# First four adjacency blocks built and widened right behind layer zero, and normalised rows and roundings moved in the adjacency loop

## What is computed

```python
x = _layernorm(x + _L0_gnn_ref(x, src, dst, W_w, W_b, a_w, a_b), axis=-1)    # attention over edges
x = _layernorm(x + _L1_gnn_ref(x, edge_index, W), axis=-1)
x = _layernorm(x + _L2_gnn_ref(x, edge_index, edge_attr_4, ...), axis=-1)    # gated messages
x = _layernorm(x + _L3_gnn_ref(x, edge_index, edge_type_64, ...), axis=-1)   # typed messages

def _L1_gnn_ref(H, edge_index, W):
    new_H = segment_sum(H[src], dst, num_segments=H.shape[0])
    return relu((H + new_H) @ W)
```

## Time and profile before

| | us |
|---|---|
| median of 3 runs | 1089.4 |
| lowest, highest | 1089.07, 1090.24 |
| the profiled execution | 1089.84 |
| its span | 1088.0 |
| PE busy | 1002.6 (92%) |
| DVE busy | 861.1 (79%) |
| ACT busy | 691.3 (64%) |
| POOL busy | 218.2 (20%) |

### The profile page before, as it was taken

One profiled execution on the slowest core, in us unless ns is written; L12 is line 12 of the kernel. 1 busy time (PEld: TensorE's weight loads), 2 busy tenths in 40 slices (PEclk: granted clock), 3 DMA queues, 4 the chain that ended last, 5 costly groups with the idle time before them and its releaser, 6 DMA issues.

```text
span 1088.0 us, 27899 instructions
## 1 busy us (share of the span) xinstructions
PE 1002.6 (92%) x10463; PEld 874.7 (80%) x10463; DVE 861.1 (79%) x1934; ACT 691.3 (64%) x1489; POOL 218.2 (20%) x260
## 2 busy tenths in 40 slices
PE   3798979699999999995999999779999999989997
PEld 3343557599999999995788889669999999976775
DVE  6875999988998989987766677788787888766754
ACT  3467765454555555456888888577677776776554
POOL 4501340000000000000000000126666666610000
PEclk9899999899999999997999999889999999999998
DMA  6000020366767677752866564235444445334232
GB/s 159 1 2 1 4 68 3 121 207 225 238 215 225 222 238 227 204 175 72 292 195 193 172 201 141 82 104 140 138 136 129 131 131 139 109 112 124 69 99 82
DMA packets 86925, 150.38 MB, mean 138 GB/s; under 512 B 14524, under 2 KB 58375, under 8 KB 86557
## 3 DMA queue, kind: packets, MB, share of 16 engines
q1 hardware_dynamic: 65609, 116.01, 35.9%
q10 hardware_dynamic: 16122, 22.16, 5.7%
q0 software_dynamic: 5056, 10.36, 3.9%
HBM read 112.56 MB, written 35.94 MB: 136 GB/s over the span
## 4 chain that ended last, share of the span: by engine, by line
PE 81%; DVE 10%; ACT 4%; issue 3%; DMA 2%; POOL 0%; POOLq 0%; DVEq 0%; SPq 0%; ACTq 0%
PE PS L2500 14%; PE PS L2705 14%; PE PS L2488 11%; PE PS L2688 8%; PE PS L2611 7%; PE PS L2791 6%; PE PS L2581 3%; PE PS L2588 3%; PE PS L2326 2%; PE PS L2339 2%; DVE ring L1659 2%; DVE vo L1663 2%; PE PS L2403 2%; ACT X L1227 1%; PE PS L2357 1%
## 5 line engine op out<-in xcount | busy, mean ns | idle before, releaser
L1151 ACT CAST vo<-XT 128x768 f32<-128x768 bf16 (+1 forms) x218 | 180.3, 827 | 163.7 <-PE PS L2705 64.2
L984 POOL DMA_INDIRECT XT<-tab,ring x158 | 159.9, 1012 | 113.5 <-PE PS L2705 60.2
L2500 PE MATMUL PS<-vo 128*128 128x133 f32 x1300 | 175.9, 284 | 1.2 <-ACT vo L1151 1.2
L2500 PEld LDWEIGHTS PS<-vo 128*128 128x128 f32 x1300 | 157.2, 191 | 1.4 <-issue 1.4
L2488 PE MATMUL PS<-kp,ring 128*128 128x132 bf16 x1950 | 146.7, 221 | 3.2 <-DVE ring L1631 1.7
L2705 PE MATMUL PS<-vo 128*128 128x128 f32 x984 | 132.8, 279 | 0.0
L2488 PEld LDWEIGHTS PS<-kp,ring 128*128 128x128 bf16 x1950 | 125.6, 97 | 5.4 <-DVE ring L1631 1.8
L1641 DVE TENSOR_TENSOR XT<-iotab,XT 128x768 bf16<-128x768 bf16 (+1 forms) x218 | 120.0, 551 | 3.2 <-DMA hots_d<-XT 1.5
L2705 PEld LDWEIGHTS PS<-vo 128*128 128x128 f32 x984 | 118.9, 191 | 3.0 <-issue 2.4
L2490 PE MATMUL PS<-SDP,ring 128*128 128x12 bf16 x650 | 110.2, 170 | 0.0
L1286 ACT CAST adjf_r<-PS 128x512 fp32r<-128x512 f32 (+1 forms) x175 | 92.4, 550 | 25.4 <-PE PS L2581 23.6
(11 more groups left out here) (350 smaller groups left out, 2008.6 us busy)
## 6 DMA issues: line engine op xcount, KB each, us to landing
ring<-rows_d SPq DMA_DIRECT2D x146, 416.0 KB, 5.8
hots_d<-XT ACTq DMA_DIRECT2D x108, 192.0 KB, 4.7
big<-hots_d SPq DMA_DIRECT2D x10, 640.0 KB, 5.3
XT<-hots_d SPq DMA_DIRECT2D x10, 640.0 KB, 4.8
adj_d<-ring SPq DMA_DIRECT2D x20, 320.0 KB, 2.4
big<-hots_d SPq DMA_DIRECT2D x8, 480.0 KB, 4.4
adj_d<-ring SPq DMA_DIRECT2D x15, 240.0 KB, 2.1
ring<-adj_d SPq DMA_DIRECT2D x11, 320.0 KB, 3.0
```

The source lines that it names most:

```text
L984: G.indirect_dma_start(far_rows[:, f % FBUF, :], None, tab[2], bass.IndirectOffsetOnAxis(ap=far_row[:, t:t + 1], axis=0)).then_inc(far_in[ ...
L1151: C.copy(ohd[:, k % 3, 0:n, :], ohb[:, k % 3, 0:n, :]).then_inc(hots_wide, 1)
L2500: T.matmul(bank(6 + b % 2)[:, 0:VW], ohd[:, k % 3, i, :], vals[:, k % 3, i, :], start=j == 0, stop=j == JN - 1).then_inc(scattered, 1)
```

## The change

Blocks 0 to 3 of layer one move forward, and rows and roundings move back.

- DVE's comparisons for `ohx` (the extra one-hots) and for `ohs` blocks 0 to 3 move into batches 103 to 106 of layer zero (`EARLY_HOTS` = 103, `AHEAD` = 4). The copy in `SLc` that they need moves into ACT's batch 101.
- PE builds blocks 0 to 3 directly behind the last scatter, once all `SUMS` copies are done, and turns `rc` behind them, into another bank.
- ACT widens the four blocks before it takes the square roots. Their byte copies stand between the normalised rows.
- ACT's rows 21 to 24 (`ACT2`), which stood before `crow`, are done one at a time behind blocks 6 to 9 of the loop (`LATE_ROWS` = 6).
- The roundings of groups 3, 4, 5 and 6 now stand behind blocks 5, 10, 12 and 14 (`rounded_at`), and DVE's subtractions of these groups in blocks 6, 11, 13 and 15.
- SP loads chunks 0 and 1 as soon as the first group's one-hots are stored; it waits for the rest before chunks 2 and 3.

```diff
+    EARLY_HOTS = HT * (NU - 1) // BT - 3
+    AHEAD = 4
+    LATE_ROWS = XBUF + 2
+
+    def rounded_at(i):
+        return XBUF + 1 if i < HBANK else LATE_ROWS + len(ACT2) + 2 * (i - HBANK)
...
-                sp.wait_ge(hots_out[r], hots_stored(r))
+                sp.wait_ge(hots_out[r], 16 * len(range(r, (len(even(0)) * JN - 1) // BT + 1, 3)))
...
+            for s in range(XBUF):
+                block_wide(s)
             for h in range(2):
                 deviations(1, h)
             act.wait_ge(scale_ready, 1)
             scaled_rows(X, range(0, QNB))
             for i in range(QBANK):
                 round_rows(1, i)
+            block_byte(0)
+            block_byte(1)
             scaled_rows(X, range(QNB, HNB - 4))
             for i in range(QBANK, HBANK - 1):
                 round_rows(1, i)
-            act.wait_ge(scale_ready, 2)
-            scaled_rows(X, ACT2)
+            block_byte(2)
+            block_byte(3)
             act.wait_ge(rc_tr, 1)
...
+                    if q == 0 and b == LATE_ROWS:
+                        act.wait_ge(scale_ready, 2)
+                    if q == 0 and 0 <= b - LATE_ROWS < len(ACT2):
+                        scaled_rows(X, [ACT2[b - LATE_ROWS]])
+                    for i in range(HBANK - 1, BANKS):
+                        if q == 0 and b == rounded_at(i):
+                            round_rows(1, i)
...
+                if k == EARLY_HOTS:
+                    dve.wait_ge(pairs_ready, 3)
+                    set_hots(0, NB, ohx[:, 0, :])
+                if 0 <= k - EARLY_HOTS < AHEAD:
+                    set_hots(0, k - EARLY_HOTS, ohs[:, k - EARLY_HOTS, :])
...
-                            if b == min(1 + i, NB - 1):
+                            if b == (1 + i if i < HBANK - 1 else rounded_at(i) + 1):
                                 dve.wait_ge(xp_top, i + 1)
...
+                if s == 0:
+                    pe.wait_ge(vals_ready, NBATCH)
+                    pe.wait_ge(sums_cp, NB)
...
-            build(0)
-            build(1)
+            for s in range(XBUF):
+                build(s)
+            pe.wait_ge(cnt_ready, 1)
+            T.transpose(bank(4)[0:NB, 0:P], rc[:, :], ident[:, :]).then_inc(rc_tr, 1)
```

More of the change, by code:

```diff
@@ L798, in _ @@
                     sp.wait_ge(hots_wide, NBATCH)
+                    for r in range(3):
+                        sp.wait_ge(hots_out[r], hots_stored(r))
                     hots_load(2)
@@ L1202, in _ @@
                 own_values(k)
+                if k == EARLY_HOTS - 2:
+                    C.copy(SLc[:, 1, :, :], SLc[:, 0, :, :]).then_inc(pairs_ready, 1)
                 if k + 1 < NBATCH:
@@ L1249, in split @@
                         C.copy(XP[:, nodes(i - 1), 1, :], AG[:, cols(i - 1)].rearrange("p (b f) -> p b f", f=F)).then_inc(xp_mid, 1)
-            C.copy(SLc[:, 1, :, :], SLc[:, 0, :, :]).then_inc(pairs_ready, 1)
             def round_rows(n, i):
@@ L1255, in round_rows, with block_wide, block_byte @@
                 C.copy(XH[:, nodes(i), :], X[:, nodes(i), :]).then_inc(xp_top, 1)
+            def block_wide(s):
+                w = even_width(s // NB)
+                act.wait_ge(adj_mm, s + 1)
+                if s >= XBUF:
+                    act.wait_ge(applied, s - XBUF + 1)
+                    dve_copied(act, s - XBUF)
+                C.copy(adjf[:, s % XBUF, 0:w], adj_bank(s)[:, 0:w]).then_inc(adjf_cp, 1)
+            def block_byte(s):
+                if not by_dve(s):
+                    adj_free(act, s)
+                    C.copy(adj_slot(s), adj_bank(s)[:, 0:even_width(s // NB)]).then_inc(adj_act, 1)
+            for s in range(XBUF):
+                block_wide(s)
             for h in range(2):
@@ L1265, in _ @@
                 round_rows(1, i)
-            act.wait_ge(scale_ready, 2)
-            scaled_rows(X, ACT2)
+            block_byte(2)
+            block_byte(3)
             act.wait_ge(rc_tr, 1)
-            C.copy(crow[:, :], bank(7)[0:NB, 0:P]).then_inc(rc_cp, 1)
+            C.copy(crow[:, :], bank(4)[0:NB, 0:P]).then_inc(rc_cp, 1)
             def rel_rows(q):
@@ L1281, in _ @@
                     s = q * NB + b
-                    act.wait_ge(adj_mm, s + 1)
                     if s >= XBUF:
[L1284 to L1291, removed]
+                        block_wide(s)
+                        block_byte(s)
+                    if q == 0 and b == LATE_ROWS:
[5 more added lines that the diff above has]
+                            round_rows(1, i)
                     if q and b == 9:
@@ L1651, in _, with set_hots @@
             FIRST = [h for h in units_at(0) if HT * h < 2 * BT]
+            def set_hots(q, j, buf):
+                V.tensor_tensor(buf.rearrange("p (k n b) -> p k n b", k=3, b=4), IN1[:, :, :].rearrange("p (k n) b -> p k n b", k=3),
+                                SLc[:, :, j, 4 * q:4 * q + 4].unsqueeze(2).to_broadcast([P, 3, NREL, 4]), ALU.is_equal).then_inc(ohs_ready, 1)
             dve.wait_ge(pool_consts, 8)
@@ L1923, in normalise @@
                     variance(1)
-                    set_hots(0, NB, ohx[:, 0, :])
                     scale(0)
@@ L1947, in split @@
                 low(BANKS - 1)
[L1949 to L1953, removed]
             normalise(1, X)
@@ L1975, in _ @@
                         dve.wait_ge(rel_mm, s - SBUF + 1)
-                    set_hots(q, b, ohs[:, s % SBUF, :])
-                    if s >= 4:
-                        adj_copy(s - 4)
+                    if s >= AHEAD:
+                        set_hots(q, b, ohs[:, s % SBUF, :])
+                    if s >= AHEAD:
+                        adj_copy(s - AHEAD)
                     if q == 0:
                         for i in range(BANKS):
-                            if b == min(1 + i, NB - 1):
+                            if b == (1 + i if i < HBANK - 1 else rounded_at(i) + 1):
                                 dve.wait_ge(xp_top, i + 1)
@@ L1985, in _ @@
                         sums_out1(q - 1)
-            for s in range(BANKS * NB - 4, BANKS * NB):
+            for s in range(BANKS * NB - AHEAD, BANKS * NB):
                 adj_copy(s)
@@ L2525, in sums @@
                     pe.wait_ge(ag_ready, BANKS)
-                    pe.wait_ge(crelT_cp, BANKS)
+                    pe.wait_ge(crel_cp, BANKS)
                     pe.wait_ge(rc_cp, 1)
@@ L2549, in _ @@
                 sums(0)
-            pe.wait_ge(cnt_ready, 1)
-            T.transpose(bank(7)[0:NB, 0:P], rc[:, :], ident[:, :]).then_inc(rc_tr, 1)
             def build(s):
@@ L2605, in apply1 @@
                     pe.wait_ge(crel_cp, q - 1)
+                if b == 0 and q == 1:
+                    pe.wait_ge(rc_cp, 1)
                 if q == 0:
```

6 lines of the change are left out of this document (3 added, 3 removed).

## The result

| | median, us | range, us | runs |
|---|---|---|---|
| before | 1089.31 | 1087.60 to 1090.96 | 14 |
| changed | 1092.59 | 1090.87 to 1093.86 | 14 |

The ratio is 1.0029, with a 95% interval of 1.0020 to 1.0037: 3.2 us slower. The forecast was 1091.6 us, slower by 2.2, with a range of 1088.3 to 1093.4.

A forecast was written before the change was run, and what follows sets the result against it. PE was taken as the bound, nearly always busy, with build 10 hanging on ACT's `crow` copy and the DMA behind it. -1.06 + 3.22 = +2.16 us gave 1091.6 us against the median, range 1088.3 to 1093.4.

The forecast's parts named there:

- Part 1: Layer zero's last batches: the moved comparisons and `SLc` copy fit; cost 0, at most 0.3 us with the cover gone.
- Part 2: First four builds, behind layer zero: the table load still ends before the variance; cost 0, cover 0.5 us.
- Part 3: Normalised rows and `crow` on ACT: `crow` copied 1.06 us earlier; first apply's head start 5.1 us.
- Part 4: Up to build 10: head start shrinks to about 2.5 us, PE waits some 2 us for chunk 2; gain 1.06 us.
- Part 5: Blocks 10 to 16: new waits make these builds take 9.02 us against 5.80 before, 3.22 us lost.
- the ring: Blocks 10 to 16: build, widen, byte copy, round, subtract, compare, next build but one; turns 3.24, 3.24, 2.54 us.
- The clock: Blocks 10 to 16: three stalls of 0.6 to 1.3 us between bursts should leave PE's clock up.
- rival 4: Clock falls in blocks 10 to 16, or moved comparisons delay layer zero: 1093.5 to 1095.5 us; chance 0.05.
- The sum: Whole kernel: -1.06 + 3.22 = +2.16 us, 1091.6 us against the median.
- The bound of 1.4 us: Load of chunk 2: upper limit of its delay if transfers shared the rate from issue; forecast added nothing for it.

The follow-up runs named there:

- e1_slack: Changed kernel with DVE's subtractions of row groups 4, 5 and 6 two blocks later (blocks 13, 15, 17); 1089.34 us, ratio 0.9997.
- e8_byte_last: Changed kernel with ACT's roundings behind blocks 10, 12 and 14 put ahead of these blocks' byte copies; 1091.39 us, ratio 1.0010.
- e5_before_ring: Kernel before with only ACT's roundings of groups 4 to 6 behind blocks 10, 12, 14 and DVE's subtractions in 11, 13, 15; 1092.64 us, ratio 1.0028.
- e10_reorder_late_chunk: Changed kernel with DVE's subtractions of groups 2 to 6 in blocks 5, 8, 13, 15, 17, chunks 2 and 3 still behind `crow`; 1091.05 us, ratio 1.0009.
- e9_fill10: Changed kernel with 34 extra identity products on PE ahead of build 10, where PE waits for the DMA; 1092.72 us, ratio 1.0027.
- e2_chunk: Changed kernel with chunks 2 and 3 loaded right behind chunks 0 and 1, ahead of the store and load of `rc`; 1089.85 us, ratio 1.0003.
- e6_reorder: Changed kernel with DVE's subtractions of groups 2 to 6 in blocks 5, 8, 13, 15, 17 and chunks 2 and 3 loaded early; 1082.93 us, ratio 0.9938.

## Why the prediction was right, point by point

- **Part 1, layer zero's tail: right.** The DVE comparisons fit: behind the second one in batch 103 the next reduction came without idle time, and the last batches run as before (that reduction comes 0.2 us late against the mark, the next one at its old place). The last `SUMS` copy started at 499.11 us; in the executions shown here it lies between 498.10 and 500.96 us, with 499.81 to 500.13 in the three of kernels whose layer zero is that of before.
- **Part 2, the early builds: right.** The table load ended 0.27 us ahead of the square root; 0.5 was taken.
- **Part 3, `crow`: right.** 1.06 us earlier was forecast, 1.09 measured (1.10 in e1_slack and e8_byte_last).
- **Part 4, the head start melts at build 10: right, its size 0.4 us off.** The wait for chunk 2 was 2.10 us (forecast some 2). From `crow` to build 10 it took 11.01 us, against 10.61 before and 10.47 to 10.61 in e1_slack, e5_before_ring, e8_byte_last and e10_reorder_late_chunk. In e1_slack the transfers are issued in the same order and at the same distances, and it took 10.61. So I take it for a scatter of this execution and no cost of the change. The advance at build 10 was 0.69 us instead of 1.06. The lower clock in this part of the forecast is 0.50 of full speed in the trace of before (each window from 506 to 518 us; 0.60 in the next).
- **Part 5, the ring: right.** 9.02 us was forecast for builds 10 to 16; at the upper clock it measured 9.13 (e9_fill10) and 9.13 (e5_before_ring), 0.11 more. The members are as named: e1_slack opens the ring at DVE, e8_byte_last shortens it by ACT's byte copy.
- **The clock: the step that failed, and a small one.** The forecast said that the stalls in the ring would leave it up. They did (1.00 in e5_before_ring and e2_chunk). But the 2 us wait for the DMA before them, which the forecast had, was not weighed for the clock, and behind it the clock fell. In the trace this is 9.54 - 9.13 = 0.41 us. It is rival 4 on a small scale, beside the forecast and not instead of it. Rival 4 priced a pair at the lower clock at 1.9 us more. Most of that was covered, since PE would have waited for the ring in that time: the fall lasted 6.8 us. Without the ring, in e1_slack, a fall half as long (3.4 us) cost 1.35 us. The fall came from the DMA's wait, as far as one trace each can tell: e1_slack has only that wait between build 7 and the fall, and in e9_fill10 that wait is filled, the ring's are left, and the clock stays up (1.00). It does not follow each time, since e8_byte_last had a wait of 1.56 us and kept its clock (1.00).
- **The sum:** -0.69 + 3.22 + 0.11 + 0.41 = +3.05 us at block 16 in the trace, forecast +2.16, measured in the runs 3.2 (2.2 to 4.0). Of the 0.89 us between forecast and trace, 0.41 is the clock, 0.37 the later chunk 2 and 0.11 the ring. In an execution without the scatter at chunk 2 the sum would be 2.7; the interval of the runs allows both.

On the order in two queues. The bound of 1.4 us for transfers that share the rate is ruled out. In e10_reorder_late_chunk the store of `adj_d` was issued 1.0 us behind the loads into `XT` (5.2 us before), and build 10 started 8.36 us after their issue (8.61 before):

```profile
515.92 0.92 SPq L785 DMA_DIRECT2D XT<-hots_d  x2
516.94 1.81 SPq L817 DMA_DIRECT2D adj_d<-ring  x1
```

So this load was not delayed by a transfer issued behind it, in this trace. And DVE passed none of the three waiting subtractions: it stood idle for 5.24, 1.53 and 1.21 us with the comparison for the next block behind each. The forecast counted the 3.22 us in full; the rows of before show DVE standing so at one place, for 0.79 us, and that it would do so at all three new ones was the author's estimate.

## What to carry to other kernels

When a step is moved to a later place of a hand-written list, look at what stands behind it in the same list. If its input depends on the newest work of the engine that waits for the next item of that list, a ring closes, and each turn is the sum of all engines' steps (3.27, 3.29 and 2.57 us in e5_before_ring, where two blocks took PE 1.93 to 1.95 before); here two places of distance in the list opened it again. And before an engine is given a head start, follow each of its next inputs back to the source: the early builds were worth 2.8 us, but only after the ring was open and the load of chunk 2 no longer hung on `crow`.

## What the runs showed of the hardware that was not expected

- The granted clock fell after a short wait in a stretch that was busy otherwise: PE idle for 2.10 us (1.69 in e1_slack), lower level (0.50) 1.2 us after work had begun again (1.4 in e1_slack), and up again 6.8 us later in the changed kernel, 3.4 in e1_slack (0.77 in the window 523 to 524, 0.52 in 526 to 527). With a wait of 1.56 us (e8_byte_last) it stayed up (1.00), as it did with idle times of 1.20, 0.85 and 0.47 us in e5_before_ring. Each is one trace, and 1.56 and 1.69 us lie too close together to show that the length of the wait alone decides.
- It rose from 0.50 to 1.00 later where PE had a break: the trace shows it 4.7 us after PE resumed where no break followed (e6_reorder), 8.2 us where a break of 1.60 us did (changed kernel; 4.5 us behind the end of that break). Taking 2.05 us of waits away there was worth 2.8 at block 16.
